# Attention block and spline-weight FFN on one core: token features spilled and loaded by halves, and the output sum moved between engines

## What is computed

```python
x = L0_attn_x                                  # (4, 1024, 512) fp32
h = layernorm(x)
q, k, v = h @ Wq, h @ Wk, h @ Wv
s = softmax(q^T k / 4)                         # 512 x 512 over features, per batch
x = x + layernorm((s @ v^T)^T @ Wo)
h = layernorm(x)
gate_w, up_w, down_w = spline(gate_cp), spline(up_cp), spline(down_cp)   # cubic, 2048 x 512 each
y = (silu(h @ gate_w^T) * (h @ up_w^T)) @ down_w^T
x = x + layernorm(y)
```

## Time and profile before

| | |
|---|---|
| median of 3 runs | 813.82 us (813.07 to 814.23) |
| the profiled execution | 809.29 us, span 807.5 us |
| PE busy | 693.4 us (86%) |
| DVE, POOL, ACT busy | 508.1, 437.3, 370.5 us |
| mean granted clock of PE | 0.93 of full speed |
| FFN block | about 394 to 807 us of the span |

### The profile page before, as it was taken

One profiled execution on the slowest core, in us unless ns is written; L12 is line 12 of the kernel. 1 busy time (PEld: TensorE's weight loads), 2 busy tenths in 40 slices (PEclk: granted clock), 3 DMA queues, 4 the chain that ended last, 5 costly groups with the idle time before them and its releaser, 6 DMA issues. The chain is left out here.

```text
span 807.5 us, 16423 instructions
## 1 busy us (share of the span) xinstructions
PE 693.4 (86%) x5872; PEld 481.9 (60%) x5872; DVE 508.1 (63%) x993; ACT 370.5 (46%) x635; POOL 437.3 (54%) x615
## 2 busy tenths in 40 slices
PE   6887999999999999799565996979969799696996
PEld 3665878787777878577322553545535455453565
DVE  7674763696368743655555585867848668573653
ACT  3532333243233323332465664756736566474651
POOL 5289768195837689104254463654626546364642
PEclk9997899999999999899677898999979999898998
DMA  6735456145713474106847145272551824627213
GB/s 234 269 103 172 147 182 214 55 150 176 260 57 120 153 258 135 46 1 209 260 130 180 30 145 157 94 196 93 146 157 65 219 97 132 157 75 178 84 60 105
DMA packets 60687, 115.01 MB, mean 142 GB/s; under 512 B 12880, under 2 KB 25296, under 8 KB 58576
## 3 DMA queue, kind: packets, MB, share of 16 engines
q1 hardware_dynamic: 60624, 114.16, 46.1%
HBM read 81.76 MB, written 32.37 MB: 141 GB/s over the span
## 5 line engine op out<-in xcount | busy, mean ns | idle before, releaser
L1270 POOL TENSOR_TENSOR act<-inter,act 128x512 f16<-128x512 f32 x128 | 156.1, 1227 | 142.7 <-ACT act L1311 142.7
L1384 DVE SCALAR_TENSOR_TENSOR inter<-ubank,c_up,gated 128x512 f32<-128x512 f32 x128 | 95.9, 750 | 101.0 <-ACT gated L1315 98.5
L1523 PE MATMUL ybank<-down,act 128*128 128x160 f16 x512 | 114.6, 242 | 0.0
L1315 ACT ACTIVATE gated<-gbank,c_gate 128x512 f32<-128x512 f32 x128 | 87.8, 686 | 58.5 <-PE gbank L1482 57.1
L1524 PE MATMUL ybank<-down,act 128*128 128x160 f16 x512 | 114.0, 241 | 0.0
L1525 PE MATMUL ybank<-down,act 128*128 128x160 f16 x512 | 113.9, 240 | 0.0
L1311 ACT CAST act<-inter 128x512 f16<-128x512 f32 x128 | 78.9, 617 | 46.9 <-DVE inter L1384 46.4
L1482 PE MATMUL gbank<-z,s_all 128*32 128x512 f16 x512 | 55.2, 422 | 43.7 <-DMA z<-token_features 33.4
L1523 PEld LDWEIGHTS ybank<-down,act 128*128 128x128 f16 x512 | 51.6, 101 | 42.8 <-issue 39.2
L1482 PE MATMUL ubank<-z,s_all 128*32 128x512 f16 x512 | 54.7, 418 | 7.8 <-DVE inter L1384 6.4
L1482 PEld LDWEIGHTS gbank<-z,s_all 128*32 128x32 f16 x512 | 13.3, 94 | 73.4 <-issue 36.7
(11 more groups left out here) (195 smaller groups left out, 1962.8 us busy)
## 6 DMA issues: line engine op xcount, KB each, us to landing
x_ln<-x SPq DMA_DIRECT2D x64, 256.0 KB, 3.3
job<-job_in SPq DMA_DIRECT2D x24, 640.0 KB, 4.8
z<-token_features SPq DMA_DIRECT2D x16, 768.0 KB, 6.2
shared<-x SPq DMA_DIRECT2D x32, 256.0 KB, 2.7
x<-shared SPq DMA_DIRECT2D x32, 256.0 KB, 2.0
token_features<-z_hi SPq DMA_DIRECT2D x64, 128.0 KB, 2.6
x_res<-x SPq DMA_DIRECT2D x32, 256.0 KB, 2.6
out<-x_res SPq DMA_DIRECT2D x32, 256.0 KB, 2.0
```

What stands on the lines that cost most here:

```text
L1270: pool.tensor_tensor(hidden[par][:, i, TOK:2 * TOK], inter[:, i % INTERS, :], hidden[par][:, i, 0:TOK], ALU.subtract).then_inc(inter_ready, 1)
L1315: act.activation(gated[:, slot % 2, :], gbank[:], ACT.Silu, scale=c_gate[:]).then_inc(silu_done, 1)
L1384: dve.scalar_tensor_tensor(out=inter[:, i % INTERS, :], in0=ubank[:], scalar=c_up[:], in1=gated[:, i % 2, :], op0=ALU.mult, op1=ALU.mult). ...
L1523: pe.matmul(out, hidden[par][:, r, high], box[:, 0], start=False, stop=False)
```

## The change

- The features are spilled and loaded by halves of the partitions (64 partitions hold 8 of the 16 feature tiles). There are 24 spills of 64 KB in place of 12 of 128 KB, with a semaphore for each half; a half's load waits for that half's spills alone. The high parts come first and wait for ScalarE (`z_hi_done`), the low parts wait for VectorE (`z_ready`). Order on SP: 12 spills of half 0, 6 of half 1, the load of half 0, the other 6 of half 1, the load of half 1.
- SP's list in an FFN group: `regroup` moves from the head of quad 2 to the end of quad 1, after `finish` of q = 0 but ahead of its `reload`; the two x1 tile loads of quad 2 move to the head of quad 1.
- `o_finish` moves from VectorE to GpSimd as a plain addition of y and the residual. The mean goes into ScalarE's `o_norm` as a bias: Identity with scale and bias in place of Copy with scale. GpSimd negates mean times deviation with one more small instruction, and `o_norm` waits for that.

```diff
-                    feats.spill(sp, 0, SPILLS // 2, 0)
+                    feats.spill(sp, 0, 0)
...
-                        feats.spill(sp, (t + 2) * SPILLS // 4, (t + 3) * SPILLS // 4, 0)
+                        feats.spill(sp, 1, 0, t * SPILLS // 2, (t + 1) * SPILLS // 2)
...
+        rows = slice(half * P // 2, (half + 1) * P // 2)
+        for n in range(first, self.SPILLS if last is None else last):
+            if half == 0 and n == 0:
+                sp.wait_ge(self.z_hi_done, (g + 1) * self.Q * 2)
+            if half == 0 and n == 2 * K:
+                sp.wait_ge(self.z_ready, (g + 1) * self.Q)
+            part, k = (1, 2, 0)[n // K], n % K
+            source = (low[rows, k, :], high[rows, k, :], high[rows, K + k, :])[part]
+            dest = self.spilled[part, k][:, half * tiles:(half + 1) * tiles, :]
+            sp.dma_start(dest.rearrange("f t n -> t f n"), source).then_inc(self.z_spilled[half], 16)
...
-        sp.wait_ge(feats.z_spilled, (g + 1) * feats.SPILLS * 16)
+        sp.wait_ge(feats.z_spilled[half], (g + 1) * feats.SPILLS * 16)
...
-                feats.spill(sp, 0, feats.SPILLS, g, 1 - par)
-                for half in range(2):
-                    ffn_in.load_z(sp, feats, g, par, half)
+                feats.spill(sp, 0, g, buf=1 - par)
+                feats.spill(sp, 1, g, 0, feats.SPILLS // 2, buf=1 - par)
+                ffn_in.load_z(sp, feats, g, par, 0)
+                feats.spill(sp, 1, g, feats.SPILLS // 2, buf=1 - par)
+                ffn_in.load_z(sp, feats, g, par, 1)
...
-                for ahead in ((0,), (1,), (2, 3), ())[j] if more else ():
+                for ahead in ((0,), (1, 2, 3), (), ())[j] if more else ():
...
-                if j == 2 and not (isinstance(g, int) and g == GROUPS - 1):
-                    regroup(g + 1, 1 - par, count)
                 for i in range(4 * j, 4 * j + 4):
                     for before, q in outputs(g, i, 2):
                         finish(before, q)
+                        if j != 1:
+                            reload(before, q)
+                if j == 1:
+                    if not (isinstance(g, int) and g == GROUPS - 1):
+                        regroup(g + 1, 1 - par, count)
+                    for before, q in outputs(g, 6, 2):
                         reload(before, q)
...
+                pool.tensor_tensor(orr[:, q, 2:3], o_zero[:], orr[:, q, 2:3], ALU.subtract).then_inc(o_mr, 1)
+            def o_finish(g, q):
+                n = held(pool, g * Q + q + 1)
+                pool.wait_ge(res2_loaded[q], held(pool, g * 16 + 16))
+                pool.wait_ge(o_normed, n)
+                pool.tensor_tensor(x_res[:, q % 2, :], y[:, q % 2, :], x_res[:, q % 2, :], ALU.add).then_inc(out_ready, 1)
...
-                act.wait_ge(o_rstd, held(act, g * Q + q + 1))
-                act.activation(y[:, q % 2, :], y[:, q % 2, :], ACT.Copy, scale=orr[:, q, 1:2]).then_inc(o_normed, 1)
+                act.wait_ge(o_mr, held(act, g * Q + q + 1))
+                act.activation(y[:, q % 2, :], y[:, q % 2, :], ACT.Identity, scale=orr[:, q, 1:2],
+                               bias=orr[:, q, 2:3]).then_inc(o_normed, 1)
...
-                dve.scalar_tensor_tensor(out=x_res[:, q % 2, :], in0=y[:, q % 2, :], scalar=orr[:, q, 2:3],
-                                         in1=x_res[:, q % 2, :], op0=ALU.subtract, op1=ALU.add).then_inc(out_ready, 1)
```

More of the change, by code:

```diff
@@ L935, in __init__, with spill @@
         self.z_ready = sem("z_ready")
-        self.z_spilled = sem("z_spilled")
+        self.z_spilled = [sem(f"z_spilled{h}") for h in range(2)]
     def load(self, sp, x1_t, m, slot):
         sp.dma_start(self.x_ln[:, slot, :], x1_t[m]).then_inc(self.ln_loaded[slot], 16)
-    def spill(self, sp, first, last, g, buf=0):
-        if first == 0:
-            sp.wait_ge(self.z_ready, (g + 1) * self.Q)
+    def spill(self, sp, half, g, first=0, last=None, buf=0):
+        K, tiles = self.K, self.spilled.shape[3] // 2
         high, low = self.z_parts[buf]
[L948 to L951, removed]
+        rows = slice(half * P // 2, (half + 1) * P // 2)
[8 more added lines that the diff above has]
+            sp.dma_start(dest.rearrange("f t n -> t f n"), source).then_inc(self.z_spilled[half], 16)
     def constants(self, pool):
@@ L975, in z_high @@
         if q == 0 and not (isinstance(groups_before, int) and groups_before == 0):
-            act.wait_ge(self.z_spilled, groups_before * self.SPILLS * 16)
+            for half in range(2):
+                act.wait_ge(self.z_spilled[half], groups_before * self.SPILLS * 16)
         for kind in range(2):
@@ L1150, in ffn_block @@
         carrier2 = sb("carrier2", [P, 1], F32)
+        o_zero = sb("o_zero", [P, 1], F32)
         gbank, ubank, tbank, zbank = [psum(n, [P, BANK], F32) for n in ("gbank", "ubank", "turned", "zbank")]
@@ L1174, in ffn_block @@
         o_rstd = sem("o_rstd")
+        o_neg = sem("o_neg")
         o_mr = sem("o_mr")
+        o_cleared = sem("o_cleared")
         o_normed = sem("o_normed")
@@ L1280, in o_scale @@
                 pool.wait_ge(o_rstd, n)
-                pool.tensor_tensor(orr[:, q, 2:3], omv[:, q, 0:1], orr[:, q, 1:2], ALU.mult).then_inc(o_mr, 1)
+                pool.tensor_tensor(orr[:, q, 2:3], omv[:, q, 0:1], orr[:, q, 1:2], ALU.mult).then_inc(o_neg, 1)
+                pool.wait_ge(o_neg, n)
+                pool.tensor_tensor(orr[:, q, 2:3], o_zero[:], orr[:, q, 2:3], ALU.subtract).then_inc(o_mr, 1)
[4 more added lines that the diff above has]
+                pool.tensor_tensor(x_res[:, q % 2, :], y[:, q % 2, :], x_res[:, q % 2, :], ALU.add).then_inc(out_ready, 1)
             def quad(g, par, count, j, made, begun, more):
@@ L1290, in quad @@
                         o_scale(before, q)
+                    for before, q in outputs(g, i, 2):
+                        o_finish(before, q)
                     if s == 1 and begun:
                         feats.scale(pool, g * Q + j + AHEAD + 1)
+            pool.memset(o_zero[:], 0.0).then_inc(o_cleared, 1)
+            pool.wait_ge(o_cleared, 1)
             pool.sem_inc(part_done, 2 * PARTS)
@@ L1301, in _ @@
             o_scale(GROUPS - 2, Q - 1)
+            o_finish(GROUPS - 2, Q - 1)
             for q in range(Q):
                 o_scale(GROUPS - 1, q)
+                if q:
+                    o_finish(GROUPS - 1, q - 1)
+            o_finish(GROUPS - 1, Q - 1)
         @block.scalar
@@ L1436, in quad @@
                         o_stats(before, q)
-                    for before, q in outputs(g, i, 2):
-                        o_finish(before, q)
                     if s == 0 and made:
@@ L1458, in _ @@
             o_stats(GROUPS - 2, Q - 1)
-            o_finish(GROUPS - 2, Q - 1)
             for q in range(Q):
@@ L1463, in _ @@
                 o_stats(GROUPS - 1, q)
-                if q:
-                    o_finish(GROUPS - 1, q - 1)
-            o_finish(GROUPS - 1, Q - 1)
         @block.tensor
```

5 lines of the change are left out of this document (removed).

## The result

Over 20 runs each on the same chip the changed kernel takes 817.38 us and the kernel before 812.09: ratio 1.0059, 95% interval 1.0044 to 1.0074. The change makes the kernel 0.6% slower; 787 us had been forecast. The profiled executions are single ones and lie further apart, 816.37 us (span 814.6) after 809.29 (807.5): that of before is 2.8 us under its median, that of after 1.0.

What follows compares the result with a forecast made beforehand. PE's 33.4 us of waits for z, behind spill, landing and load, were taken as the bound. Stalls -19.2, clock -8.5 and end +1.1 summed to -26.6: 787 us from the 813.8 median, range 770 to 815.

Steps and rivals of the forecast that it cites:

- the end: End of the span: negation, about 0.5 us, and a sum of 1.29 in place of 0.75 add 1.1 us.
- The start of the spill: SP at a regrouping: the first spill goes out 2.5 us earlier, bounds 2.0 to 3.1.
- The cadence of a half: SP's spill issues: one half each 0.51 us, bounds 0.47 to 0.645; eighteen take 9.2 us plus 0.6.
- (b): Rival on SP's spill issue: a half costs what a whole one costs, cadence 0.645, 812.5 us; chance 0.11.
- The residual of q = 2: SP's list: its load moves from 521.2 to about 534, needed about 538; cover some 5 us.
- the move of the sum: Output sum from VectorE to GpSimd: 1.29 + 0.3 us more per quad there, covered; gain nothing, 0 to 0.5 a quad.
- Clock: PE behind the z stalls: no clock fall where 1 to 2 us idle remain, gaining 8.5 us, bounds 0 to 12.
- The attention block: Twelve more issues, 6 us, between x1 stores are absorbed by SP's 11.1 us of idling: 0, to +1.
- `o_norm`'s hold: ScalarE's o_norm waits some 0.3 to 0.5 us longer, but its next cast waits for VectorE anyway: nothing.
- the prediction's signs of being wrong: In the new profile: L951 at 0.60 or longer, spills landing after 4 us, PE waiting on act, GpSimd's sum on q = 2's residual.
- The mild form of (c): At the z load: only the load lands 1.5 us late, 5 x 1.5 off the gain, 796 us; chance 0.03.
- (c): Rival on the DMA engines: halves drain too slowly, the z load starts or lands late; 822.6 us at 0.72 each; chance 0.14.

Runs made afterwards that it cites:

- e14: The change with 12 whole spills instead of halves, high parts still first, new SP order, sum on GpSimd: 798.41 us, ratio 0.9854 to the kernel before.
- e13: The kernel before with SP's new order and high parts spilled first; 12 whole spills, sum on VectorE: 788.78 us, ratio 0.9706 to before.
- e6: The changed kernel with the residual load of q = 2 right behind the 12 spills of half 0: 814.99 us, ratio 1.0034 to before.
- e9: The kernel before with SP's new order and the sum on GpSimd; 12 whole spills, high parts not first: 800.51 us, ratio 0.9860 to before.
- e10: The changed kernel with the sum back on VectorE and the residual of q = 2 loaded behind half 0's spills: 805.39 us, ratio 0.9932 to before.
- e11: The changed kernel with the first group's features, in the attention block, spilled in 12 whole pieces: 815.86 us, ratio 1.0043 to before.
- e7: The changed kernel with ScalarE scaling by Copy, without mean bias or wait for the negation: 816.73 us, ratio 1.0053 to before.
- e1: The kernel before with only the sum moved to GpSimd, with negation and bias; spills and SP's order unchanged: 822.1 us, ratio 1.0102 to before.

## Why the prediction was wrong

The measured 817.38 us lie above the stated range of 770 to 815. The prediction took 3.3 us off a stall: 2.5 at the start of the spill, 0.5 between the first spill and the load, and 0.3 at the load. On the means of the five periods the start came 1.2 us earlier, first spill to load became 1.3 us *longer*, and load to gate became 0.2 shorter, so nothing came off. The step that failed is the cost of the eighteen issues; beside it stand four terms that were put at nothing or nearly nothing (the late residual, the first group's spills, the hold of ScalarE, the end) and the gain of clock that hung on shorter stalls.

**The start of the spill: right in kind, half in size.** 2.5 us earlier was forecast, and 1.2 came. Store to first spill fell by 3.08 us, and the store came 1.91 later. Of that about 1.1 had been forecast for the sum on GpSimd, and e14 against e13 measures just that (29.49 and 28.40). Of the rest, 0.74 goes when the residual is early (e6).

**The cadence of a half: the step that failed.** 0.51 us was taken, from 0.427 + 0.04 and 0.517 + 0.04; it is 0.615, near the far end of the bounds. The 18 issues take 11.1 us where 9.8 were forecast. Rival (b) had the size, from the 64-row store in the earlier trace rows, and it was given 0.11: the row with the same number of partitions was the nearest one, and I took a mean of two others. With whole spills the same path takes 10.1 to 10.4 us (e9, e13, e14): the halves save the wait for landing, 1.8 us, and pay 3.7 us in issues for it. The rule that I set against the change, in the Trainium skill, "DMA: Bandwidth & Descriptors", section "Rules for kernel authors", not to split a transfer into partition halves, holds here by its outcome: the change is 2.05% slower than e14, its like with whole spills. What the traces show of the price is SP's issues and what they push back; whether both halves run on the same engines, which is the reason that the page gives, no run here shows.

**The residual of q = 2: "about 534, needed about 538", cover 5 us, cost 0.** It went out at 545.40: I had counted the spills and loads that it is moved past, but not that SP also stands for half 1's landing, 3.9 us of it; the rest is the later store and the longer cadence. After, GpSimd waits 8.55 us for it at that place:

```profile
551.95 1.27 POOL L1307 TENSOR_TENSOR x_res<-y,x_res 128x512 f32<-128x512 f32 x1 [8.55 <-DMA x_res<-x]
```

Its price by itself is 0.25% with the sum on GpSimd (e6, not clear of noise) and 2.1% with the sum on VectorE (e10). Here the part of the change that I priced at nothing, the move of the sum, does do something: it shields VectorE. It gives less than it costs once the halves are gone (e14 and e13).

**Clock: -8.5 forecast, next to nothing came.** I had expected stalls of 1 to 2 us; they stayed at 2.75 to 3.5, and 6.0 at the last. Windows behind the gate at 542.08, answering to the earlier trace rows:

```profile
542.00:544.00 2.00, 1.92 (x17) 0.57 (x18) 0.53 (x1) 1.25 (x2) 1.40 (x2) 0.52 0.27 86
544.00:546.00 2.00, 2.00 (x21) 2.00 (x22) 0.22 (x1) 0.75 (x2) 0.00 (x0) 0.62 0.57 102
```

0.52 and 0.62 as before, that is, mostly the lower of the two levels, 1.2 GHz. Only behind one of the seven gates, at 591.50 after a stall of 3.33 us, did the clock stay at 1.00. Whether stalls of 1 to 2 us leave the clock up, e13 shows in part. Three of its stalls are 1.98, 0.91 and 2.12 us long, at the gates at 442.41, 485.85 and 629.20; the windows behind them:

```profile
442.41:444.41 2.00, 2.00 (x18) 0.63 (x19) 0.61 (x1) 0.69 (x1) 1.34 (x2) 0.50 1.09 258
485.85:487.85 2.00, 2.00 (x32) 1.36 (x33) 1.91 (x8) 1.51 (x3) 1.41 (x5) 1.00 1.00 238
629.20:631.20 2.00, 2.00 (x32) 1.37 (x33) 1.19 (x2) 1.30 (x2) 1.88 (x4) 1.00 1.02 228
```

The clock stayed up behind two of the three and fell behind one, so the length of a stall alone did not settle it, and stalls of 1 to 2 us might have won only a part of the 8.5 us.

**The attention block: 0 to +1 forecast, 4.5 later at the first gate.** SP's idle time of 11.1 us there did take up the six more microseconds of issues, as the earlier trace rows let one expect (4.6 us of it are left after); what was late were the last x1 stores, above all by their landing (e11). I had looked at SP's waits and not at what else the DMA engines carry in that stretch.

**`o_norm`'s hold: nothing forecast, 0.63 us a quad where nothing else holds the quad up.** "Its next cast waits for VectorE anyway" is false in the last group: the cast stands behind `o_norm` on ScalarE, and the silu behind the cast (e7). With +1.1 forecast, the end took +5.4: some 3.1 for the sum (e14's last group 70.1 us, e13's 67.0), this hold among it, and some 2.6 for the late residual (e6).

**The rivals.** (b) was the nearest in its mechanism and in its time, 812.5, and left out the residual and both ends. One of the prediction's signs of being wrong came true as well, GpSimd's sum waiting on the residual of q = 2. (The mild form of (c) is 794.7 by its own sum, not 796.) (c), halves that drain too slowly, is not what happened to the first load: it went out 0.13 us behind the last issue ahead of it, so nobody waited for a landing there. SP did wait for half 1, whose last spills land beside the load of half 0; whether that load holds them up or the halves themselves are slow was not tried. Waits of SP's list, after:

```profile
SPq L1098 <- DMA token_features<-z_lo: 28.4, 7, 4.3
```

How many of the 16 DMA engines a half uses stays open.

**That e13 comes at 788.78 us, near the 787 of the forecast, is not a confirmation of it:** it has the early start that I reckoned with, its 12 issues and the wait for landing take 10.35 us, not far from the 9.8 that I gave to 18 halves, and it pays neither for the sum nor for a residual as late as the change's. That the two numbers meet is luck.

## What to carry to other kernels

Before splitting a transfer to let its reader start sooner, count the issues that now stand ahead of that reader, at the price of a whole one, and every later transfer of the same list: here 18 issues in place of 12 cost more than the wait for landing that they saved, and a residual that left 20 us later behind the same store (22.0 us in place of 2.2) cost another 2.1% where VectorE waited for it. A move between engines that "hides" has two prices to look for, what it holds up in front of a store that a queue waits for, and what stands behind the new wait on a third engine, and the second shows only in the stretch where nothing else is late. When a change bundles an order, a split and a move, time them apart: here the order alone was worth 1.8%, with the high parts first 2.9%, and the other parts took it all back.

## What the runs showed of the hardware

A spill of 64 KB from 64 partitions holds SP for 571 ns and one of 128 KB from 128 partitions for 604: for this transfer, half the size saved 5% of the issue. An addition of two 128x512 fp32 operands takes GpSimd 1.27 us (VectorE's form of it took 1.22 on the mean). Where that work is off VectorE, GpSimd's `low` takes less time: 1227 ns on the mean before, 1177 after, and 1160 in e1, where nothing but the sum is moved. ScalarE's 128x512 scaling takes 720 ns as Copy with a scale and 812 as Identity with scale and bias, both taken from `orr`.
